# Four-stage convolution network on one core: identity and group matrix kept on chip, the last stage's constants loaded a stage earlier

## The reference

```python
x = x + L0(_gn(x))   # locally connected 3x3 (own weights per pixel), batch norm, relu
x = x + L1(_gn(x))   # modulated deformable 3x3 convolution: offsets and gates from a 3x3 convolution, bilinear gather
x = x + L2(_gn(x))   # spatial attention map from mean and max over channels, masked region norms, gamma and beta from 7x7 convolutions
x = x + L3(_gn(x))   # linear attention over all C*H*W tokens with per-token weights, then a per-token tanh layer
```

## Time and profile before

| | |
|---|---|
| median of 3 runs | 3220.82 us (3220.05 to 3222.2) |
| the profiled execution, own time | 3215.99 us |
| span of its trace, first to last instruction | 3214.2 us |
| PE busy | 1549.9 us (48%) |
| DVE busy | 1985.6 us (62%) |
| ACT busy | 854.6 us (27%) |
| POOL busy | 1777.7 us (55%) |
| mean DMA traffic | 150 GB/s over the span |

### The profile page before, as it was taken

How to read it: one execution, slowest core, us unless ns; L and a number is a source line. 1 busy time by engine, 2 the same in 40 slices (tenths; PEclk the granted TensorE clock), 3 DMA queues, 4 the chain that set the end, 5 groups by cost and what they waited for, 6 DMA issues and landing times. The chain is left out here.

```text
span 3214.2 us, 31625 instructions
## 1 busy us (share of the span) xinstructions
PE 1549.9 (48%) x11604; PEld 893.3 (28%) x11604; DVE 1985.6 (62%) x1764; ACT 854.6 (27%) x1110; POOL 1777.7 (55%) x1353
## 2 busy tenths in 40 slices
PE   3665551222222222222222220263888888888897
PEld 3454420000100001000110000151454555555555
DVE  4222235555545455555555555575999999999995
ACT  2111151111111111111111100154454454444441
POOL 2000027777777777777777777334544544545542
PEclk8778765555555555555555555586999999999999
DMA  9999863655445554555445553313122212212212
GB/s 371 406 429 429 362 161 118 160 154 142 133 135 150 148 136 132 136 151 147 135 131 138 153 144 104 130 31 95 57 66 92 91 65 93 90 65 100 83 63 92
DMA packets 337893, 483.66 MB, mean 150 GB/s; under 512 B 186016, under 2 KB 277940, under 8 KB 320048
## 3 DMA queue, kind: packets, MB, share of 16 engines
q1 hardware_dynamic: 279120, 330.24, 30.3%
q0 software_dynamic: 58720, 152.72, 16.7%
HBM read 397.28 MB, written 85.45 MB: 150 GB/s over the span
## 5 line engine op out<-in xcount | busy, mean ns | idle before, releaser
L438 POOL DMA_INDIRECT gath<-table,idx x1152 | 1217.0, 1056 | 430.5 <-issue 368.3
L613 DVE TENSOR_TENSOR gath<-gath,p_stat 128x2304 f32<-128x2304 f32 x128 | 327.0, 2554 | 745.9 <-DMA gath<-table,idx 643.5
L650 PE MATMUL p_z<-wz,pairs 128*128 128x384 f32 x384 | 262.2, 814 | 450.6 <-issue 447.3
L496 ACT ACTIVATE zt<-p_z 128x384 f32<-128x384 f32 x192 | 93.4, 492 | 981.2 <-remote 604.7
L650 PEld LDWEIGHTS p_z<-wz,pairs 128*128 128x128 f32 x384 | 98.8, 296 | 602.6 <-issue 591.2
L1269 PE MATMUL p_state<-xt,tri 128*128 128x512 f32 x512 | 239.4, 611 | 41.0 <-DVE prod L1158 40.9
L640 PE MATMUL p_conv<-sides,wconv 128*128 128x512 f32 x64 | 66.3, 1139 | 398.0 <-issue 236.1
L1049 POOL TENSOR_TENSOR gated<-gated,outw 128x512 f32<-128x512 f32 x64 | 124.2, 1946 | 210.0 <-ACT gated L1102 210.0
L1158 DVE TENSOR_TENSOR prod<-p_state,query 128x2048 f32<-128x2048 f32 x80 | 182.2, 2277 | 54.1 <-PE p_state L1274 51.5
L1035 POOL TENSOR_TENSOR query<-query,expo 128x2048 f32<-128x2048 f32 x16 | 72.5, 4534 | 254.3 <-DVE expo L1131 254.3
L658 PE MATMUL p_y<-ident,yt 128*128 128x128 f32 x64 | 17.8, 433 | 389.6 <-DVE yt L621 389.6
(11 more groups left out here) (232 smaller groups left out, 3161.2 us busy)
## 6 DMA issues: line engine op xcount, KB each, us to landing
ring<-in_w SPq DMA_DIRECT2D x64, 2304.0 KB, 19.3
hidw<-in_hidw SPq DMA_DIRECT2D x64, 1024.0 KB, 5.2
table<-zt SPq DMA_DIRECT2D x256, 144.0 KB
table<-zt SPq DMA_DIRECT2D x512, 72.0 KB
gath<-table,idx POOLq DMA_INDIRECT x1152
xt<-in_x SPq DMA_DIRECT2D x4, 1024.0 KB, 8.0
resid<-xt SPq DMA_DIRECT2D x32, 128.0 KB, 2.3
xlate<-resid SPq DMA_DIRECT2D x16, 256.0 KB, 2.8
```

The costliest lines, as they stand in the source:

```text
L438: nc.gpsimd.indirect_dma_start(out=gath[:, t % SLOTS, k].rearrange("p n c -> p (n c)"), out_offset=None, in_=tables[u], in_offset=bass.Ind ...
L613: tt(g, g, w, ALU.mult).then_inc(weighted, 1)
L650: nc.tensor.matmul(p_z[i % ZS][:], pairs[u][:, 4 * J:4 * J + 4].rearrange("p j w -> p (j w)"), wz[:, m * WIDE:(m + 1) * WIDE], start=True, ...
```

## The change

`ident` and `gnmat` become tiles of the whole program. Stage 1 loads them as before, and stages 2 to 4 use them from there, so that three loads of each go. The seven other constants of stage 4 join the `EARLY` list and are loaded in stage 3 behind `inw` and `inb`; their tiles lie outside stage 3's. Stage 3's own constants are issued in another order, and PE's wait for them stands ahead of the first map convolution instead of ahead of the group chain. In stage 4 PE waits for `EARLY` where it waited for `consts_in`, and SP's first action is the wait for the saving of x.

```diff
@@ layer1 @@
-        ident = sb("ident", [P, P]); gnmat = sb("gnmat", [P, P])
-            for name, tile in (("bnmat", bnmat), ("affine0", affine), ("gnmat", gnmat)):
+            for name, tile in (("bnmat", bnmat), ("affine0", affine)):
                 sp.dma_start(tile[:], d[name][:]).then_inc(bn_in, 16)
-            for name, tile in (("wconv", wconv), ("wz", wz), ("ident", ident), ("base", base), ("obias", obias),
+            for name, tile in (("wconv", wconv), ("wz", wz), ("base", base), ("obias", obias),
                                ("place_of", place_of)):
-                    act.wait_ge(consts_in, 96)
+                    act.wait_ge(consts_in, 80)
-            dve.wait_ge(bn_in, 48)
+            dve.wait_ge(bn_in, 32)
-            pe.wait_ge(bn_in, 48)
+            pe.wait_ge(bn_in, 32)
             join_groups_tensor(nc, pe, bnmat[:], bn["mv"][:, 0, 0:1], 1, bn, gs, 2)
             join_groups_tensor(nc, pe, gnmat[:], gn["mv"][:, 0:FIRST, 0], FIRST, gn, gs, 3)
-            pe.wait_ge(consts_in, 96)
+            pe.wait_ge(consts_in, 80)
@@ layer2 @@
-            for name, tile in (("gnmat", gnmat), ("bnmat", bnmat), ("ident", ident), ("band", band), ("mbias", mbias)):
+            for name, tile in (("band", band), ("mbias", mbias), ("bnmat", bnmat)):
                 sp.dma_start(tile[:], d[name][:]).then_inc(consts_in, 16)
             tiles, early_in = early
             for name, tile in tiles.items():
-            pe.wait_ge(consts_in, 80)
             join_groups_tensor(nc, pe, gnmat[:], gn["mv"][:, :, 0], B, gn, gs, 5)
             pe.wait_ge(zeroed, 3)
+            pe.wait_ge(consts_in, 48)
             pe.wait_ge(pooled_ready, 1)
@@ EARLY @@
-EARLY = {"inw": [P, 3 * ATT, HALF], "inb": [P, 3 * ATT, HALF]}
+EARLY = {"inw": [P, 3 * ATT, HALF], "inb": [P, 3 * ATT, HALF], "tri": [P, P], "pick": [P, ATT + 1, 32], "give": [P, ATT + 1, P],
+         "outb": [P, HALF], "edge": [P, 2], "hidb": [P, ATT, HALF], "outw": [P, ATT, HALF]}
@@ layer3 @@
-            sp.dma_start(gnmat[:], d["gnmat"][:]).then_inc(gnmat_in, 16)
-            for name, tile in (("ident", ident), ("tri", tri), ("pick", pick), ("give", give), ("edge", edge),
-                               ("hidb", hidb), ("outw", outw), ("outb", outb)):
-                sp.dma_start(tile[:], d[name][:]).then_inc(consts_in, 16)
             sp.wait_ge(saved, 16 * (2 * B + 1))
-            pool.wait_ge(consts_in, 128)
-            dve.wait_ge(consts_in, 128)
-            pe.wait_ge(gnmat_in, 16)
             join_groups_tensor(nc, pe, gnmat[:], gn["mv"][:, :, 0], B, gn, gs, 6)
-            pe.wait_ge(consts_in, 128)
+            pe.wait_ge(early_in, 16 * len(EARLY))
@@ build_program @@
+        ident, gnmat = (whole.enter_context(nc.sbuf_tensor(name, [P, P], F32)) for name in ("ident", "gnmat"))
```

More of the change, by code:

```diff
@@ L87, in stat_buffers, with layer0 @@
     return t
-def layer0(nc, xt, d, row_stats, tables, gs):
+def layer0(nc, xt, d, row_stats, tables, gs, ident, gnmat):
     NQ, PX = 4, 8
@@ L117, in layer0 @@
         bias = sb("bias0", [P, HALF])
-        gnmat = sb("gnmat0", [P, P])
         sums = sb("sums0", [P, 2, W // G, P])
@@ L121, in layer0 @@
         turn = ctx.enter_context(nc.psum_tensor("turn0", [P, W, QUAD], F32))
-        ident = sb("ident0", [P, P])
         x_in = [sem(f"x_in{i}") for i in range(PARTS)]; consts_in = sem("consts_in")
@@ L313, with layer1 @@
 NT = H * W // P
-def layer1(nc, xt, d, row_stats, tables, gs):
+def layer1(nc, xt, d, row_stats, tables, gs, ident, gnmat):
     SLOTS = NT
@@ L677, with layer2 @@
 THRESHOLD = 0.8
-def layer2(nc, xt, d, early, row_stats, resid, saved, gs):
+def layer2(nc, xt, d, early, row_stats, resid, saved, gs, ident, gnmat):
     N = B * H * W
@@ L701, in layer2 @@
         lower = [sb(f"lower{u}", [P, HALF]) for u in range(2)]
-        band = sb("band", [P, 12, P]); ident = sb("ident", [P, P]); gnmat = sb("gnmat", [P, P]); bnmat = sb("bnmat", [P, P])
+        band = sb("band", [P, 12, P]); bnmat = sb("bnmat", [P, P])
         ones = sb("ones", [P, P]); mbias = sb("mbias", [P, 2])
@@ L902, in early_tiles, with layer3 @@
     return tiles, ctx.enter_context(nc.semaphore("early_in"))
-def layer3(nc, xt, d, out, early, row_stats, resid, saved, gs):
+def layer3(nc, xt, d, out, early, row_stats, resid, saved, gs, ident, gnmat):
     A = ATT
@@ L912, in layer3 @@
     tiles, early_in = early
-    inw, inb = (tiles[name] for name in EARLY)
+    inw, inb, tri, pick, give, outb, edge, hidb, outw = (tiles[name] for name in EARLY)
     with ExitStack() as ctx:
@@ L922, in sem @@
             return ctx.enter_context(nc.semaphore(name + "_3"))
-        hidb = sb("hidb", [P, A, HALF]); outw = sb("outw", [P, A, HALF]); outb = sb("outb", [P, HALF])
-        ident = sb("ident", [P, P]); tri = sb("tri", [P, P]); gnmat = sb("gnmat", [P, P])
-        pick = sb("pick", [P, TERMS, LANE]); give = sb("give", [P, TERMS, P]); edge = sb("edge", [P, 2])
         kv = xt[:].rearrange("p (j i) x -> p j i x", i=A)
@@ L950, in layer3 @@
         slots = out.rearrange("b (k m p) -> b m k p", k=4, p=P)
-        consts_in = sem("consts_in"); gnmat_in = sem("gnmat_in"); own_dve = sem("own_dve"); norm_done = sem("norm_done")
+        own_dve = sem("own_dve"); norm_done = sem("norm_done")
         x_in = sem("x_in"); late_in = sem("late_in"); out_done = sem("out_done")
@@ L1362, in build_program @@
     with nc.sbuf_tensor("xt", [P, B, HALF], F32) as xt, nc.sbuf_tensor("row_stats", [P, B, 6], F32) as row_stats, ExitStack() as whole:
+        ident, gnmat = (whole.enter_context(nc.sbuf_tensor(name, [P, P], F32)) for name in ("ident", "gnmat"))
         gs = {name: whole.enter_context(nc.semaphore(f"norm_{name}")) for name in STAT_SEMS}
         tables = [nc.dram_tensor(f"table{u}", (TAPS * WP * WP + 1, 2 * C), F32, kind="Internal").ap() for u in range(2)]
-        layer0(nc, xt, d, row_stats, tables, gs)
-        layer1(nc, xt, d, row_stats, tables, gs)
+        layer0(nc, xt, d, row_stats, tables, gs, ident, gnmat)
+        layer1(nc, xt, d, row_stats, tables, gs, ident, gnmat)
         with ExitStack() as ctx:
@@ L1370, in build_program @@
             saved = ctx.enter_context(nc.semaphore("saved"))
-            layer2(nc, xt, d, early, row_stats, resid, saved, gs)
-            layer3(nc, xt, d, out, early, row_stats, resid, saved, gs)
+            layer2(nc, xt, d, early, row_stats, resid, saved, gs, ident, gnmat)
+            layer3(nc, xt, d, out, early, row_stats, resid, saved, gs, ident, gnmat)
 def layouts(inp):
```

## The result

The changed kernel's median is 3213.77 us over 10 runs, against 3222.67 us over 10 runs of the kernel before on the same chip. The ratio is 0.9970, with a 95% interval of 0.9962 to 0.9979. That is 9 to 10 us faster, where 16.1 us were predicted, and the time lies above the stated range. Three further comparisons of the unchanged pair gave 0.9972, 0.9972 and 0.9975. The ratios leave out a few executions in a slower state (4769.1 us of the kernel before, 3486.77 and 5024.87 us of `x7_one_memset`), while the medians are over all.

What follows compares the result with a forecast made beforehand. POOL's gathers fill stage 2 and DVE stage 4, both untouched; gains come at seams where PE waits for DMAs. 1.0 + 5.2 + 1.9 + 8.0 = 16.1 us off 3220.82 gives 3204.7 us, range 3200.7 to 3209.5.

Steps and rivals of the forecast that it cites:

- Stage 2, 1.0 us: Start of stage 2: without gnmat PE waits only until affine0 lands, gaining 1.0 us, bounds 0.5 and 1.0.
- Stage 4, 8.0 us: Start of stage 4: PE's turn no longer waits for outb, so it comes 8.0 us earlier, 0.64 for gnmat included.
- The rival of a stretch there: Stage 4: a 3.8 us stretch like stage 3's shows once the outb wait is gone, leaving 12.3 us; chance 0.10.
- a hold by another wait: Stage 4: another wait holds the first projection until its old time, leaving 8.1 us of gain; chance 0.04.
- The rival of slower gathers: Stage 2's gather loop: moved tile addresses add 30 ns per gather, 34.6 us in all, giving 3239.3 us; chance 0.08.
- Stage 3, 5.2 + 1.9 us: Head of stage 3: PE starts 5.2 us earlier without its DMA wait, and half the chain's 3.8 us stretch goes.
- The bound "0 of the stretch goes": Stage 3's chain: lower bound where all 3.8 us of stretch stay but the 5.2 us still count; sum 13.7 us.
- SP's third issue, 1.31 us long: Head of stage 3: a slow DMA issue at 2054.93, read as stretch already present before the large loads are queued.
- The large loads meet the chain: Stage 3: loads issued sooner stretch the chain by the removed wait's 5.2 us, leaving 9.0 us, 3211.8; chance 0.06.
- The page's rule: Stage 3's chain: code fetched after a taken branch makes the engine wait, so the stretch stays and its term is 0.
- The median: Whole kernel: the runs' median lies 4.8 us above the profiled execution, a difference carried over to the forecast.

Runs made afterwards that it cites:

- x7_one_memset: Changed kernel with one added 6.88 us memset of xn on DVE ahead of stage 3's statistics; ratio 0.9979, median 3103.25 us.
- b_again: The kernel before, unchanged, run again for a profile on the same chip as the changed kernel; 3220.1 us in one run.
- y1_seven_in_stage4: Changed kernel with the seven constants loaded at the head of stage 4 again, ident and gnmat still resident; ratio 0.9961, median 3096.65 us.
- a_ctrl: The changed kernel, unchanged, run again on one chip with the kernel before; ratio 0.9972, median 3208.04 us.
- after_again: The changed kernel run again, unchanged, as partner of three variants on one chip; ratio 0.9972, median 3205.99 us.
- a_third: The changed kernel, unchanged, run once more beside the repeat with a memset ending stage 2; ratio 0.9975, median 3209.02 us.
- x2_table_early_b: Repeat of x2_table_early: changed kernel with a square root ending ACT's stage 2, moving its table load there; ratio 0.9968, median 3206.34 us; first run 3094.66 us.
- e3_wait_back: Changed kernel with PE's wait for stage 3's three constants put back ahead of the chain; ratio 0.9974, median 3207.92 us.
- e1_early_after_chain: Changed kernel with SP issuing the nine EARLY loads only after stage 3's norm_done; ratio 0.9973, median 3206.28 us.
- e2_all_after_chain: Changed kernel with SP issuing every stage 3 DMA, band, mbias and bnmat included, only after norm_done; ratio 0.9969, median 3205.84 us.
- x4_delay_in_stage2_c: Third run of the changed kernel with one memset of gath (15.4 us) on DVE at the very end of stage 2; 3213.92 us.
- x1_delay_in_stage3_b: Second run of the changed kernel with three 6.88 us memsets of xn on DVE ahead of stage 3's statistics; 3224.16 us.
- x6_memsets_later: Changed kernel with POOL's three memsets at stage 3's head held until the first normalised image; 3096.5 and 3088.61 us in single runs.

## Why the prediction was wrong

**Stage 2, 1.0 us: right within its bounds.** PE's first matmul moved by 0.99 us against the statistics, by the landing of `affine0` as worked out. Against `b_again` it moved by 0.52, the lower bound: the 2.3 us that `gnmat` took to land were that execution's. Up to the first gather 0.8 us are left in this profile; in the other profiles that head scatters by about 1 us.

**Stage 4, 8.0 us: right.** 7.99 us, with the new neighbour of the turn as named. The turn follows ACT by 0.15 us, where 0.04 were expected. The rival of a stretch there did not show (chain 3.15 us), nor did a hold by another wait. `y1_seven_in_stage4` splits the term: 6.4 us for the seven loads, the rest for `gnmat` and for two DMAs fewer ahead of `outb`.

**The rival of slower gathers** did not come: three of the four profiles of the changed kernel have 1584.5 or 1584.6 us from first to last gather, like the kernel before.

**Stage 3, 5.2 + 1.9 us: wrong, and this is the step that failed.** It said that with nothing to wait for PE starts 0.1 us after DVE, and that 0 to 3.8 us of the chain's stretches go besides, so 5.2 us were held to be certain and only the stretch open. Measured: the head became 0.8 us longer instead of 7.1 shorter in the first pair of profiles, and kept its length between `b_again` and `a_ctrl` on one chip (14.16 and 14.17 us). Counted from the last gather, which takes account of stage 3 beginning 0.7 us sooner in `b_again` (12.9 us after it and not 13.6), ACT's first image comes 0.7 to 0.8 us later in all four profiles of the changed kernel. The bound "0 of the stretch goes" left out that the stretch could take back the removed wait too. I took the stretch for a length added to the chain, when it is a period that ends at a time of its own. In the kernel before, the chain began late in that period and met less of it (6.99 and 7.61 us); in the changed kernel it begins earlier and meets more (9.15 to 9.87 us).

That reading fits every profile of the kind with the stretch. The time from the start of the last gather to ACT's first image:

| kernel | last gather | first image | between |
|---|---|---|---|
| before | 2040.47 | 2067.54 | 27.1 |
| b_again | 2042.45 | 2069.52 | 27.1 |
| after | 2048.21 | 2076.08 | 27.9 |
| after_again | 2040.56 | 2068.34 | 27.8 |
| a_ctrl | 2040.03 | 2067.81 | 27.8 |
| a_third | 2043.15 | 2070.93 | 27.8 |
| x2_table_early_b | 2043.51 | 2071.28 | 27.8 |
| e3_wait_back | 2040.98 | 2068.75 | 27.8 |
| e1_early_after_chain | 2040.95 | 2068.02 | 27.1 |
| e2_all_after_chain | 2040.39 | 2067.47 | 27.1 |
| x4_delay_in_stage2_c | 2040.43 | 2075.90 | 35.5, chain not stretched |
| x1_delay_in_stage3_b | 2042.40 | 2086.37 | 44.0, chain not stretched |

PE's start lies anywhere from 4.3 to 6.6 us after the stage's statistics, and the end takes one of two values, 0.7 us apart. `x1_delay_in_stage3_b` and `x4_delay_in_stage2_c` show the other side: 30 us and more after the last gather the same chain takes 3.2 us. This is shown. What keeps the hand-overs slow for so long after the last gather has landed is not. One sign that the prediction read for a stretch was none: SP's third issue, 1.31 us long, takes 1.81 us in `x4_delay_in_stage2_c`, where the chain is not stretched.

**The rival with the right number had the wrong cause.** "The large loads meet the chain" gave 9.0 us and 3211.8 us, close to what was measured. But `e2_all_after_chain` has the stretch with no load in flight, and delaying the early loads gave 0.7 us, not 5.2. That the number came near is luck as far as the loads go; what the rival had right is that the stretch grows by what the removed wait gave.

**The page's rule.** By "Runtime: NRT & Kernel Launch", section "Instruction fetch mechanics", of the Trainium skill the stretch would belong to code that has to be fetched after a branch. `x4_delay_in_stage2_c` enters the same code of stage 3 and has no stretch, and neither has any of the eight profiles of the second kind. The traces do have rows for fetched code, the instruction queues. These are the queues' rows in `e2_all_after_chain` from the start of stage 3's statistics to ACT's first image (2054 to 2067), and then in `y1_seven_in_stage4` over the same part (1950.8 to 1955.3).

```profile
q8 instruction: 1, 0.02, 0.4%
```

```profile
q1 hardware_dynamic: 427, 1.21, 88.6%
q8 instruction: 1, 0.02, 2.0%
```

Both move one packet of 0.02 MB there, and the chain takes 9.14 us in the one and 3.17 in the other. A fetch in the head does not by itself make the stretch, so that rule does not explain it here.

**What was never in the estimate: two kinds of measurement.** The kernels were timed in several sets, each with the kernel before beside the others, and the sets differ in a way that has nothing to do with the kernels. In the first set and three later ones the kernel before takes 3216 to 3223 us, the gathers take 1584.5 us in all profiles but one, and stage 3's chain is stretched unless it is put off. In two sets the kernel before takes 3109 to 3111 us, the gathers of the profiled kernels take 1481 to 1487 us, and the chain takes 3.15 to 3.17 us in all eight profiles. Chip number 1 stands under a set of each kind, so it is not a property of a chip that I can name. The second kind allows estimates of what the change is worth without the stretch. Edits that cost next to nothing were faster than the kernel before by 16.3 us (`x2_table_early`) and 14.5 and 20.0 us (`x6_memsets_later`, twice) in single runs. `x7_one_memset` makes 6.5 + 8.6 = 15.1 us when its delay is taken off, and `y1_seven_in_stage4` makes 12 + 6.4 = 18.4 us with the seven loads put back, each with some 4 us either way. So the predicted 16 us may well hold where there is no stretch, but the changed kernel was not timed there, and this stays open.

**The median.** I carried the profile's distance to the median over. The kernel before came out 1.9 us higher over its ten runs than over the first three (3222.67 for 3220.82). That is a fifth of the 9.1 us by which the predicted time was missed; the rest is the missed gain, 8.9 us for 16.1.

## What to carry to other kernels

A stretch in a chain of hand-overs is either a length that travels with the instructions or a period that ends at its own time. Before a removed wait is counted as gained, ask what the released instructions will run in; with a period the gain is bounded by its end, and the bound for "the stretch stays" must include that it grows by the whole wait. A delay put ahead of the chain, long enough to outlast the period, tells the two apart in one profile (here 17.5 us did). It has to be run where the undelayed kernel shows the stretch.

A load moved from the head of a stage into an earlier stage with an idle queue gave all that the timeline promised, because its wait ended last and the next waits in line could be read off and had long been met.

## What the hardware showed that I had not expected

In the kind with the stretch, POOL's gathers keep a beat too, but only in bursts. Here are four that follow each other in such a burst of `a_ctrl`, and then three in `x6_memsets_later_b`, of the kind without it.

```profile
1519.23 1.79 POOL L435 DMA_INDIRECT gath<-table,idx  x1 [0.30 <-issue]
1521.33 1.09 POOL L435 DMA_INDIRECT gath<-table,idx  x1 [0.30 <-issue]
1522.73 1.10 POOL L435 DMA_INDIRECT gath<-table,idx  x1 [0.30 <-issue]
1524.13 1.10 POOL L435 DMA_INDIRECT gath<-table,idx  x1 [0.30 <-issue]
```

```profile
1514.86 0.94 POOL L435 DMA_INDIRECT gath<-table,idx  x1 [0.30 <-issue]
1516.11 0.96 POOL L435 DMA_INDIRECT gath<-table,idx  x1 [0.30 <-issue]
1517.38 0.95 POOL L435 DMA_INDIRECT gath<-table,idx  x1 [0.30 <-issue]
```

The first come 2.10, 1.40 and 1.40 us apart, all multiples of 0.70; the others 1.25 and 1.27. The beat is not the rule of the loop: in `a_ctrl` 693 of the 1151 distances from gather to gather are 1.30 us or less, and 211 lie within 0.03 us of 1.40. In `x6_memsets_later_b` these are 1033 and 5. The bursts begin at about 780 us. The first 240 distances add up to 312.9 and 310.2 us in the two profiles, and behind them the mean is 1.40 us against 1.29, which makes up nearly all of the 100 us between the two kinds.

SP's DMAs at the head of stage 3 stand 0.70 and 1.40 apart in the same kind, and the chain's hand-overs 1.40. First to last gather lies within 0.2 us of 1584.5 us in eleven of the twelve profiles of that kind. Issuing a gather, issuing a DMA and passing a semaphore thus seem to queue for one thing that serves at a fixed beat, in bursts during the gathers and for some 27 us after the last one is issued. That is an inference from the equal spacing; no run isolated it, and no run shows what starts the bursts.
